# Shared-key attention on one core: transposed products in three banks, maxima turned on DVE, plain scores issued first

## Chip, cores and metric

The kernel runs on one core of one Trainium2 chip. The metric is the device time of one execution in microseconds, from runs of the compiled program; lower is better. The kernel before takes 4062.18 us, the median of three runs (4059.2 to 4066.68).

## What is computed

The reference is four transformer layers over x of shape [4, 512, 512]; each adds an attention and then a feed-forward part to x. The change touches the attention of the last two layers only, which is the same in both: 32 query heads of width 16 share 8 key/value heads, and keys and values are the context itself.

```python
def _L2_xattn_ref(q, k, v):
    NUM_Q_HEADS = 32
    NUM_KV_HEADS = 8
    ...
    qh = q.reshape(B, S, KV, G, D).transpose(0, 2, 3, 1, 4)
    kh = k.reshape(B, S, KV, D).transpose(0, 2, 1, 3)
    vh = v.reshape(B, S, KV, D).transpose(0, 2, 1, 3)
    scores = jnp.einsum('bkgsd,bktd->bkgst', qh, kh) / scale
    weights = jax.nn.softmax(scores, axis=-1)
    out = jnp.einsum('bkgst,bktd->bkgsd', weights, vh)
    return out.transpose(0, 3, 1, 2, 4).reshape(b, s, E)
```

The call adds this to x: `x = x + _L2_xattn_ref(_layernorm(x, axis=-1), ctx_512, ctx_512)`, and the same for layer 3.

## The kernel before

`stage_attend_shared` (L1385) is built twice, as at2 and at3. A **group** is one key/value head of one of the four batches with its four query heads, so there are 32 groups in a stage. A group has 16 **pairs** n = 0 to 15, each a tile of 128 tokens and one head, over 512 tokens.

Every score is made twice. The **plain** score of a pair (`scores`, L1521, matmul L1529) has queries down the partitions, and only serves to find each query's maximum over the keys: two pairs, n = 2m and 2m+1, fill one of two PSUM tiles of two banks, `score[m % 2]`, and DVE reduces the set m in one instruction (`max_set`, L1645, L1648). So pair 2m waits on PE until DVE has reduced set m - 2 (`maxed`). The **transposed** score (`scores_T`, L1534, matmul L1540) has keys down the partitions. Its query operand `qT` carries two more rows, the maxima split in a high and a low part, which meet rows of -1 in `kT`; so the maximum is already subtracted. ACT takes the exponential of each out of PSUM (L1628) into `probs`. Two banks, `scoreT[n % 2]`, serve the transposed products, so the one of pair n waits for the exponential of pair n - 2 (`exped`). The plain score of a pair sits in one half of the array's rows and the transposed one of the same pair in the other half.

`results(g, place, t)` (L1543, L1553) multiplies the four `probs` of one tile with the values, the fourth block of a group being issued in the next slot after pair LAST; such four products are called a results block below. ACT copies the accumulated result out (`move_res`, L1620), PE turns it with four transpositions (`turn_results`, L1565) into bank 7, and DVE divides by the sums (`finish`, L1661: a reciprocal L1663 and a product L1666).

The maxima take this path: DVE splits them (`split_maxima`, L1655, L1657), PE turns them by four transpositions into bank 7 as well (`turn_max`, L1560), ACT copies eight rows to `maxT` (`move_max`, L1615), and SP writes them with four DMAs into `qT` (`put_max`, L1495).

The order of work is written out by hand. One **slot** s does the transposed scores and results of group s and the plain scores and reductions of group s + 2. On PE a slot runs over the pairs, and these lines set it:

```python
    LAST, VALUES, MAX, RES = 1, (5, 9, 13), 5, 9
    ...
                    scores_T(s, place, j, n)
                    if ahead >= 2:
                        scores(s + 2, place + 2, j, n)
                    if n == LAST and not first:
                        results(s - 1, place + 3, TB - 1)
                    if n in VALUES:
                        results(s, place, VALUES.index(n))
```

`turn_max` stands after pair 5 (MAX) and `turn_results` after pair 9 (RES). On DVE a slot is the split of group s + 1's maxima, then eight reductions, with `finish(s - 1)` after the reduction of set (RES + 1) // 2 = 5. On SP a slot is the twelve loads of group s + 3 and then the four DMAs of `put_max`. Slots 1 to 24 run in a loop whose body holds eight of them; slots 30 and 31 have no plain scores.

Of the kernel before, what the change touches and what calls it, by code (L numbers as in the profile page):

```python
# [1384 lines left out]
def stage_attend_shared(k, nm, ctx_g, q_hi, q_lo, k_hi, k_lo, factor, queries):  # L1385
# [12 lines left out]
    LAST, VALUES, MAX, RES = 1, (5, 9, 13), 5, 9  # L1398
    with stage_room(k) as room:
        ctx, block = room.memory, room.block  # L1400

        def sb(name, shape, dt=F32):
# [8 lines left out]
        maxima, inv = sb("maxima", [P, TB, H]), sb("inv", [P, TB, H])  # L1411
        split = [sb(f"split{r}", [P, TB, P // 2, 2], F32R) for r in range(2)]
        maxT = [sb(f"maxT{r}", [2 * H, S]) for r in range(2)]
# [3 lines left out]
        (cleared, consts, spilled, scored, maxed, max_split, turned_max, max_moved, scoredT, exped, valued, vals_kept, res_moved, turned_res,  # L1417
         inv_made, finished, added) = k.sems(
            ctx, nm, "cleared consts spilled scored maxed max_split turned_max max_moved scoredT exped valued vals_kept res_moved turned_res "
# [29 lines left out]

        @block.vector  # L1450
        def _(dve):
            for r in range(SLOTS):
                dve.memset(kT[r][:, :].bitcast(F32), -1.0).then_inc(cleared, 1)
            for r in range(2):
                dve.memset(vals[r][:, :, :], 0.0).then_inc(consts, 1)
                dve.memset(split[r][:, :, :, :].bitcast(F32), 0.0).then_inc(consts, 1)
            dve.wait_ge(consts, 4)
# [13 lines left out]
        def _(sp):  # L1471
# [15 lines left out]
            def put_max(place, j, g):  # L1487
# [15 lines left out]
            put_max(0, 0, 0)  # L1503
            sp.wait_ge(spilled, 2 * B * DMA)

            def slot(s, place, j, ahead):
                if ahead >= 3:
# [3 lines left out]
                if ahead >= 1:  # L1511
                    put_max(place + 1, j, s + 1)
# [4 lines left out]
        def _(pe):  # L1517
# [16 lines left out]
            def scores_T(g, place, j, n):  # L1534
# [4 lines left out]
                pe.wait_ge(exped, PAIRS * g + n + 1)  # L1539
                pe.matmul(scoreT[n % 2][:, :], kT[r][half(h % 2, USED + 2), t * P:(t + 1) * P], qT[r][half(h % 2, USED + 2), h // 2, :],  # L1540
# [15 lines left out]
            def turn_max(g, place):  # L1556

                pe.wait_ge(max_split, 2 * (g + 1))
# [1342 lines left out]
```

## Time and profile before

| | |
|---|---|
| median of three runs | 4062.18 us |
| the profiled execution's own time | 4080.94 us |
| its span on the core | 4079.3 us |
| PE busy | 3337.4 us (82%) |
| DVE busy | 2324.2 us (57%) |
| ACT busy | 1934.3 us (47%) |
| granted PE clock over the span | 0.91 of full |
| reductions L1648, 512 of them | 623.9 us busy, 259.5 us idle before them |
| exponentials L1628, 1024 of them | 568.4 us busy, 368.0 us idle before them |
| transposed scores L1540, 1024 of them | 452.1 us busy, 177.8 us idle before them |

The shares are means over stages with other limits; the two attention stages run from about 1775 to 2276 us and from about 3140 to 3659 us of the span. The numbers behind a group of instructions are its busy time and the time that its engine stood idle just before one of them. A timeline row gives start and length in us, and in brackets the idle time of the engine before it and what ended it. The granted clock is 1.00 at 2.4 GHz and 0.50 at 1.2 GHz.

### The profile page before, as it was taken

The page shows a single profiled execution, that of the slowest core. Times are in us where ns is not written, and L with a number is a line of the kernel's source. Part 1 is how long each engine was busy: PE and PEld are TensorE (multiplying, and loading weights), DVE is VectorE, ACT ScalarE, POOL GpSimd, SP SyncE. Part 2 cuts the span into 40 slices and gives each one's busy share as a digit, 9 for nine tenths or more (in the row PEclk, how much of TensorE's full clock was granted, in tenths as well). Part 3 has the DMA queues.
Part 4 walks back from the last instruction along what each step waited for, and adds up shares of the span by engine and source line. Part 5 has one row for each costly group of instructions (what it writes and reads, how often), then busy time and mean ns, then how long its engine had stood idle before and what let it go on. Part 6 is the DMA issues. An engine that isn't in the chain of part 4 may idle for free. (4 is left out here: it accounts for less than half of the span.)

```text
span 4079.3 us, 62234 instructions
## 1 busy us (share of the span) xinstructions
PE 3337.4 (82%) x17174; PEld 2276.6 (56%) x17174; DVE 2324.2 (57%) x3679; ACT 1934.3 (47%) x3331; POOL 606.2 (15%) x901
## 2 busy tenths in 40 slices
PE   3359996899871999668888689899897788878998
PEld 2137775666551788533332367888775233326886
DVE  6954445455443343477777444566567676745565
ACT  5643333355530555346666433566433566654333
POOL 2410001544223000210000030122111000000000
PEclk7669998999985999869999799999997999989999
DMA  3424442400011333341111152567443211102223
GB/s 137 147 98 139 139 138 89 165 0 0 11 52 62 111 119 107 111 152 43 42 41 32 70 183 93 193 242 240 167 141 119 71 40 41 42 21 67 96 94 113
DMA packets 174475, 404.47 MB, mean 99 GB/s; under 512 B 28484, under 2 KB 28612, under 8 KB 173682
## 3 DMA queue, kind: packets, MB, share of 16 engines
q1 hardware_dynamic: 141010, 286.47, 22.0%
q0 software_dynamic: 22480, 96.23, 6.9%
q10 hardware_dynamic: 10864, 20.45, 1.3%
q8 instruction: 41, 0.67, 0.1%
q14 instruction: 80, 0.66, 0.1%
HBM read 312.32 MB, written 87.03 MB: 98 GB/s over the span
## 5 line engine op out<-in xcount | busy, mean ns | idle before, releaser
L1648 DVE TENSOR_REDUCE at_maxima<-psum 128x2 f32<-128x1024 f32 x512 | 623.9, 1223 | 259.5 <-PE psum L1529 241.8
L1628 ACT ACTIVATE at_probs<-psum 128x512 f32<-128x512 f32 x1024 | 568.4, 595 | 368.0 <-PE psum L1540 337.6
L1540 PE MATMUL psum<-at_qT,at_kT 50*128 50x512 f32 x1024 | 452.1, 491 | 177.8 <-ACT at_probs L1628 167.7
L1540 PEld LDWEIGHTS psum<-at_qT,at_kT 50*128 50x128 f32 x1024 | 175.9, 192 | 496.9 <-ACT at_probs L1628 438.6
L1529 PE MATMUL psum<-at_kT,at_qT 48*128 48x512 f32 x1024 | 431.4, 496 | 14.6 <-DVE at_maxima L1648 12.4
L573 PE MATMUL psum<-f_xT_hi,ffn_w_hi 128*128 x1024 | 406.8, 397 | 9.9 <-DVE f_xT_lo L313 2.8
L573 PE MATMUL psum<-f_xT_lo,ffn_w_hi 128*128 x1024 | 405.9, 396 | 0.0
L1553 PE MATMUL psum<-at_probs,at_vals 128*32 128x512 f32 x2048 | 292.7, 640 | 0.0
L590 PE MATMUL psum<-ffn_w_hi,ffn_hid_hi 128*128 128x512 f32 x768 | 269.3, 391 | 1.3 <-ACT ffn_hid_hi L636 1.3
L387 PE MATMUL psum<-ident,n_normed 128*128 128x128 f32 x448 | 95.5, 389 | 195.9 <-ACT n_normed L353 159.3
L478 ACT ACTIVATE ffn_w_hi<-ffn_w_raw 128x512 fp32r<-128x512 f32 x262 | 161.6, 633 | 157.3 <-PE psum L595 100.1
L573 PEld LDWEIGHTS psum<-f_xT_hi,ffn_w_hi 128*128 128x128 f32 x1024 | 194.0, 189 | 56.7 <-issue 12.1
L486 DVE TENSOR_TENSOR ffn_w_lo<-ffn_w_raw,ffn_w_hi 128x512 fp32r<-128x512 f32 x262 | 176.7, 686 | 76.1 <-ACT ffn_w_hi L478 75.9
L573 PEld LDWEIGHTS psum<-f_xT_lo,ffn_w_hi 128*128 128x128 f32 x1024 | 193.9, 189 | 44.5
L595 PE MATMUL psum<-ffn_w_hi,ffn_hid_lo 128*128 128x512 f32 x768 | 205.3, 389 | 0.0
L1325 DVE TENSOR_REDUCE at_maxima<-psum 128x1 f32<-128x128 f32 (+3 forms) x256 | 122.5, 489 | 141.9 <-PE psum L1135 138.3
L573 PE MATMUL psum<-f_xT_hi,ffn_w_lo 128*128 x512 | 202.5, 396 | 0.0
L592 PE MATMUL psum<-ffn_w_lo,ffn_hid_hi 128*128 128x512 f32 x512 | 199.5, 390 | 0.0
L387 PEld LDWEIGHTS psum<-ident,n_normed 128*128 128x128 f32 x448 | 79.8, 204 | 212.0 <-issue 147.8
L1529 PEld LDWEIGHTS psum<-at_kT,at_qT 48*128 48x128 f32 x1024 | 170.8, 194 | 28.5 <-DVE at_maxima L1648 22.7
L676 DVE TENSOR_TENSOR n_normed<-n_normed,psum 128x512 f32<-128x512 f32 (+1 forms) x88 | 60.4, 687 | 217.2 <-ACT n_normed L633 211.0
L1296 ACT ACTIVATE at_probs<-psum 128x512 f32<-128x512 f32 (+3 forms) x256 | 111.9, 438 | 136.9 <-PE psum L1149 136.7
(399 smaller groups left out, 7354.9 us busy)
## 6 DMA issues: line engine op xcount, KB each, us to landing
ffn_w_raw<-in_stream SPq DMA_DIRECT2D x262, 256.0 KB, 2.7
ffn_w_hi<-quantized SPq DMA_DIRECT2D x66, 512.0 KB, 3.5
ffn_w_hi<-quantized SPq DMA_DIRECT2D x65, 256.0 KB
at_qT<-q_hi SPq DMA_DIRECT2D x256, 64.0 KB, 2.2
ffn2a_w_raw<-in_shared2a SPq DMA_DIRECT2D x26, 512.0 KB
ffn2b_w_raw<-in_shared2b SPq DMA_DIRECT2D x26, 512.0 KB
qz_raw<-in_stream SPq DMA_DIRECT2D x17, 768.0 KB, 4.2
quantized<-qz_quant POOLq DMA_DIRECT2D x16, 768.0 KB, 3.5
```

The source lines that it names most:

```text
L387: mm = pe.transpose(turned_ps[u][:, c, :], normed[u][:, c * P:(c + 1) * P], k.ident[:, :])
L478: act.activation(hi[slot][:, :], raw[slot][:, :], ACT.Copy).then_inc(made, 1)
L486: dve.tensor_tensor(lo[slot][:, :], raw[slot][:, :], hi[slot][:, :].bitcast(F32), ALU.subtract).then_inc(made, 1)
L573: mm = pe.matmul(hid_ps[h][s][0:n, :], wt[s][:, w], xt[:, c, bass.ds(b * S, S)], start=(c == 0 and i == 0), stop=(c == DC - 1 and i == len ...
L590: pe.matmul(out[t][:, :], hid_hi[s][0:n, tok], w2_hi[s][0:n, :], start=first, stop=False)
L592: pe.matmul(out[t][:, :], hid_hi[s][0:n, tok], w2_lo[s][0:n, :], start=False, stop=False)
L595: mm = pe.matmul(out[t][:, :], hid_lo[s][0:n, t * P:(t + 1) * P], w2_hi[s][0:n, :], start=False, stop=last)
L1529: mm = pe.matmul(score[m % 2][:, 512 * (n % 2):512 * (n % 2) + S], qT[r][half(par, USED), jj, t * P:(t + 1) * P], kT[r][half(par, USED), : ...
L1540: pe.matmul(scoreT[n % 2][:, :], kT[r][half(h % 2, USED + 2), t * P:(t + 1) * P], qT[r][half(h % 2, USED + 2), h // 2, :], start=True, sto ...
L1553: pe.matmul(res[h * OW:(h + 1) * OW, :], vals[place % 2][:, t, :], probs[n % RING][:, :], start=(t == 0), stop=(t == TB - 1), tile_positio ...
L1628: act.activation(probs[n % RING][:, :], scoreT[n % 2][:, :], ACT.Exp, scale=factor).then_inc(exped, 1)
L1648: dve.tensor_reduce(maxima[:, t, 2 * jj:2 * jj + 2], score[m % 2].rearrange("p (h s) -> p h s", h=2), AX.X, ALU.max).then_inc(maxed, 1)
```

## The change

Three things change in `stage_attend_shared`; line numbers below that are not of the kernel before are those of the changed one.

1. Transposed products rotate through three banks, 4 to 6 (`turn_of`). `res` moves to bank 7. The turned results no longer have a bank of their own: they take the bank of the rotation that would be pair 8's, between pair 7 and pair 10. So pair n waits for the exponential of pair n - 3 (n - 2 for pairs 0, 1, 8, 9), and pair 10 waits for `finish`.
2. The maxima are turned on DVE, by a transposition of 32x32 blocks (L1652) into `across`. SP writes that to a DRAM scratch `tops` (`send_max`, L1495), waits for the landing, and `put_max` (L1506) gathers from `tops` into `qT` in four DMAs. PE's four transpositions and ACT's copy per group are gone.
3. The plain score of pair n is issued ahead of the transposed one. The positions in a slot are now LAST = 2, VALUES = (6, 10, 14), RES = 7, and `finish` follows the reduction of set (7 + 1) // 2 = 4.

```diff
-    LAST, VALUES, MAX, RES = 1, (5, 9, 13), 5, 9
+    LAST, VALUES, MOVE, RES = 2, (6, 10, 14), 2, 7
+    TURNS = 3
...
-        score, scoreT, res, turn = [room.psum[:, 1024 * m:1024 * m + 1024] for m in range(2)], room.banks[4:6], room.banks[6], room.tiles(7)
+        score, scoreT, res = [room.psum[:, 1024 * m:1024 * m + 1024] for m in range(2)], room.banks[4:4 + TURNS], room.banks[7]
+        turn = room.tiles(4 + (RES + 1) % TURNS)
...
+        def turn_of(n):
+
+            return (n if n <= RES else n + 1) % TURNS
...
+            def send_max(place, g):
+
+                sp.wait_ge(max_turned, g + 1)
+                sp.dma_start(tops[place % SLOTS, :, :], across[place % 2][:, :]).then_inc(max_out, DMA)
+
...
-                sp.wait_ge(max_moved, g + 1)
+                sp.wait_ge(max_out, DMA * (g + 1))
+                rows = tops[r, :, :].rearrange("(b h o t) i -> h o t b i", b=TB, h=H, o=2)
                 for jj in range(2):
                     for par in range(2):
                         at = HALF * par + USED
-                        row0 = 2 * (2 * jj + 1 - par)
-                        sp.dma_start(qT[r][at:at + 2, jj, :].bitcast(F32), maxT[place % 2][row0:row0 + 2, :]).then_inc(put[r], DMA)
+                        dst = qT[r][at:at + 2, jj, :].bitcast(F32).rearrange("o (t b i) -> o t b i", t=TB, b=TB)
+                        sp.dma_start(dst, rows[2 * jj + 1 - par]).then_inc(put[r], DMA)
...
             def slot(s, place, j, ahead):
+                if ahead >= 1:
+                    send_max(place + 1, s + 1)
                 if ahead >= 3:
...
-                pe.wait_ge(exped, PAIRS * g + n + 1)
-                pe.matmul(scoreT[n % 2][:, :], kT[r][half(h % 2, USED + 2), t * P:(t + 1) * P], qT[r][half(h % 2, USED + 2), h // 2, :],
+                if n < 2:
+                    pe.wait_ge(exped, PAIRS * g + n + 1)
+                elif n > 2:
+                    pe.wait_ge(exped, PAIRS * g + (n + 1 if RES < n < RES + TURNS else n))
+                if n == RES + TURNS and not is_first(g):
+                    pe.wait_ge(finished, g + 1)
+                pe.matmul(scoreT[turn_of(n)][:, :], kT[r][half(h % 2, USED + 2), t * P:(t + 1) * P], qT[r][half(h % 2, USED + 2), h // 2, :],
...
-                    scores_T(s, place, j, n)
                     if ahead >= 2:
                         scores(s + 2, place + 2, j, n)
+                    scores_T(s, place, j, n)
                     if n == LAST and not first:
                         results(s - 1, place + 3, TB - 1)
                     if n in VALUES:
                         results(s, place, VALUES.index(n))
-                    if n == MAX and ahead >= 1:
-                        pe.wait_ge(max_moved, s + 1)
-                        if not first:
-                            pe.wait_ge(finished, s)
-                        turn_max(s + 1, place + 1)
                     if n == RES and not first:
                         pe.wait_ge(res_moved, s)
-                        if ahead >= 1:
-                            pe.wait_ge(max_moved, s + 2)
-                        else:
-                            pe.wait_ge(finished, s)
+                        pe.wait_ge(exped, PAIRS * s + n + 1)
                         turn_results()
...
-                    if n == MAX + 1 and ahead >= 1:
-                        move_max(s + 1, place + 1, j)
...
+                if not (isinstance(g, int) and g < 2):
+                    dve.wait_ge(max_out, DMA * (g - 1))
+                dve.transpose(across[place % 2][:, :], split[:, :, :, :].rearrange("p h o t -> p (h o t)").bitcast(F32)).then_inc(max_turned, 1)
```

PE in the middle of a slot of the kernel before; L1540 is the transposed and L1529 the plain score, L1553 the results, L1565 the turned results. The rows begin with the two scores of pair 9:

```order
L1540 MATMUL psum<-at_qT,at_kT 128x512
L1529 MATMUL psum<-at_kT,at_qT 128x512
L1553 MATMUL psum<-at_probs,at_vals 32x512 x4
L1565 MATMUL psum<-ident,at_resT 128x128 x4
L1539 REGISTER_ALU
L1540 MATMUL psum<-at_qT,at_kT 128x512
L1528 REGISTER_ALU
L1529 MATMUL psum<-at_kT,at_qT 128x512
L1539 REGISTER_ALU
L1540 MATMUL psum<-at_qT,at_kT 128x512
L1529 MATMUL psum<-at_kT,at_qT 128x512
```

The same place in the changed kernel, where L1559 is the transposed and L1543 the plain score, L1572 the results and L1577 the turned results. The rows begin just behind the turning that follows pair 7, with pairs 8, 9 and 10, and end with a results block and the plain score of pair 11:

```order
L1542 REGISTER_ALU
L1543 MATMUL psum<-at_kT,at_qT 128x512
L1556 REGISTER_ALU
L1559 MATMUL psum<-at_qT,at_kT 128x512
L1543 MATMUL psum<-at_kT,at_qT 128x512
L1556 REGISTER_ALU
L1559 MATMUL psum<-at_qT,at_kT 128x512
L1542 REGISTER_ALU
L1543 MATMUL psum<-at_kT,at_qT 128x512
L1559 MATMUL psum<-at_qT,at_kT 128x512
L1572 MATMUL psum<-at_probs,at_vals 32x512 x4
L1543 MATMUL psum<-at_kT,at_qT 128x512
```

Before, a results block stood behind the odd pair of a set, so both plain scores of the set were out; now it stands behind the even pair, and the odd pair's plain score comes after the block. The last transposed score shown, pair 10's, is the one that waits for `finish`.

DVE in the changed kernel, from the split and the new transposition at a slot's head to `finish` (L1657, L1660) and the reduction behind it:

```order
L1646 CAST at_split<-at_maxima 128x4x4
L1647 ISA
L1648 TENSOR_TENSOR at_split<-at_maxima,at_split 128x4x4
L1649 REGISTER_ALU
L1651 REGISTER_ALU
L1652 STREAM_TRANSPOSE at_across<-at_split 128x32
L1638 REGISTER_ALU
L1639 TENSOR_REDUCE at_maxima<-psum 128x2 x2
```

```order
L1639 TENSOR_REDUCE at_maxima<-psum 128x2
L1657 RECIPROCAL at_inv<-psum 128x16
L1660 TENSOR_TENSOR at_result<-psum,at_inv 128x256
L1638 REGISTER_ALU
L1639 TENSOR_REDUCE at_maxima<-psum 128x2
```

`finish` moved ahead by one reduction, from behind the sixth to behind the fifth, and the transposition is new.

## Rows read from the trace of the kernel before

**Rows 1.** All transposed scores: count, ns min/median/max, first and last start.

```profile
L1540 PE MATMUL psum<-at_qT,at_kT x1024: 386/495/793, 1793.3 to 3655.0; 50*128 50x512 f32 x171
```

**Rows 2.** PE's timeline, 1904 to 1926 us: start, length, engine, line, tiles, idle before.

```profile
1904.36 0.50 PE L1529 MATMUL psum<-at_kT,at_qT 48*128 48x512 f32 x1
1904.79 1.06 PE L1553 MATMUL psum<-at_probs,at_vals 128*32 128x512 f32 x8
1905.78 0.66 PE L1565 MATMUL psum<-ident,at_resT 128*128 128x128 f32 x4
...
1906.37 0.73 PE L1529 MATMUL psum<-at_kT,at_qT 48*128 48x512 f32 x2
...
1910.66 0.50 PE L1540 MATMUL psum<-at_qT,at_kT 50*128 50x512 f32 x1 [0.45 <-ACT at_probs L1628]
...
1925.19 0.50 PE L1540 MATMUL psum<-at_qT,at_kT 50*128 50x512 f32 x1 [0.45 <-ACT at_probs L1628]
```

**Rows 3.** DVE's timeline, 1904 to 1909 us.

```profile
1904.92 1.23 DVE L1648 TENSOR_REDUCE at_maxima<-psum 128x2 f32<-128x1024 f32 x1 [0.65 <-PE psum L1529]
1907.18 1.23 DVE L1648 TENSOR_REDUCE at_maxima<-psum 128x2 f32<-128x1024 f32 x1 [1.04 <-PE psum L1529]
1908.33 0.25 DVE L1663 RECIPROCAL at_inv<-psum 128x16 f32<-128x16 f32 x1
1908.61 0.42 DVE L1666 TENSOR_TENSOR at_result<-psum,at_inv 128x256 f32<-128x256 f32 x1
```

**Rows 4.** Timeline of all engines at 1789 us, before slot 0.

```profile
1789.08 2.36 DVE L1648 TENSOR_REDUCE at_maxima<-psum 128x2 f32<-128x1024 f32 x2 [0.40 <-PE psum L1529]
...
1790.36 0.80 PE L1529 MATMUL psum<-at_kT,at_qT 48*128 48x512 f32 x2 [0.82 <-DVE at_maxima L1648]
```

**Rows 5.** Groups by line, 1910.6 to 1925.2 us: busy, mean ns, idle before.

```profile
L1648 DVE TENSOR_REDUCE at_maxima<-psum 128x2 f32<-128x1024 f32 x9 | 11.0, 1224 | 3.9 <-PE psum L1529 3.4
```

**Rows 6.** SP's timeline of the same slot: the first load, the four puts.

```profile
1910.39 0.34 SPq L1482 DMA_DIRECT2D at_qT<-q_hi  x1
...
1918.38 2.43 SPq L1495 DMA_DIRECT2D at_qT<-at_maxT  x4
```

**Rows 7.** PE's timeline at three longer waits.

```profile
1928.33 0.78 PE L1540 MATMUL psum<-at_qT,at_kT 50*128 50x512 f32 x1 [1.16 <-ACT at_probs L1628]
...
3304.78 0.50 PE L1540 MATMUL psum<-at_qT,at_kT 50*128 50x512 f32 x1 [1.19 <-ACT at_probs L1628]
...
3424.88 0.50 PE L1540 MATMUL psum<-at_qT,at_kT 50*128 50x512 f32 x1 [0.99 <-ACT at_probs L1628]
```

**Rows 8.** Stretches behind them: us, busy (PE, PEld, DVE, ACT, POOL), PEclk, DMA, GB/s.

```profile
1928.40:1935.20 6.80, 6.53 (x24) 2.65 (x24) 2.45 (x2) 3.04 (x6) 0.00 (x0) 0.50 0.19 49
...
3307.40:3310.70 3.30, 3.30 (x16) 1.31 (x16) 1.22 (x1) 0.60 (x1) 0.00 (x0) 0.50 0.06 20
...
3426.90:3437.00 10.10, 9.63 (x36) 3.55 (x38) 3.93 (x4) 3.85 (x8) 0.00 (x0) 0.50 0.06 17
```

**Rows 9.** PE's timeline in slot 30 of at3, where no plain scores are.

```profile
3628.38 0.79 PE L1540 MATMUL psum<-at_qT,at_kT 50*128 50x512 f32 x1
3629.10 1.93 PE L1553 MATMUL psum<-at_probs,at_vals 128*32 128x512 f32 x8
3630.97 1.12 PE L1565 MATMUL psum<-ident,at_resT 128*128 128x128 f32 x4
```

**Rows 10.** PE's timeline: slot 30 and last turning of at2, slot 0, 30, last turning of at3.

```profile
2240.12 0.90 PE L1540 MATMUL psum<-at_qT,at_kT 50*128 50x512 f32 x2 [0.54 <-ACT at_probs L1628]
...
2275.85 0.66 PE L1565 MATMUL psum<-ident,at_resT 128*128 128x128 f32 x4 [0.69 <-ACT at_resT L1620]
...
3170.56 0.79 PE L1540 MATMUL psum<-at_qT,at_kT 50*128 50x512 f32 x1 [9.78 <-DMA at_qT<-at_maxT]
...
3618.34 0.90 PE L1540 MATMUL psum<-at_qT,at_kT 50*128 50x512 f32 x2 [0.54 <-ACT at_probs L1628]
...
3658.40 0.66 PE L1565 MATMUL psum<-ident,at_resT 128*128 128x128 f32 x4 [0.69 <-ACT at_resT L1620]
```

More of the change, by code:

```diff
@@ L1455, in _ @@
                 dve.memset(vals[r][:, :, :], 0.0).then_inc(consts, 1)
-                dve.memset(split[r][:, :, :, :].bitcast(F32), 0.0).then_inc(consts, 1)
-            dve.wait_ge(consts, 4)
+            dve.wait_ge(consts, 2)
             for r in range(2):
@@ L1554, in results @@
                               start=(t == 0), stop=(t == TB - 1), tile_position=(0, h * OW), skip_group_check=True).then_inc(valued, 1)
-            def turn_max(g, place):
-                pe.wait_ge(max_split, 2 * (g + 1))
-                for t in range(TB):
-                    mm = pe.transpose(turn[:, t, :], split[place % 2][:, t, :, :].rearrange("p c o -> p (c o)").bitcast(F32), k.ident[:, :])
-                mm.then_inc(turned_max, 1)
             def turn_results():
@@ L1566, in turn_results @@
                 mm.then_inc(turned_res, 1)
-            pe.wait_ge(consts, 6)
+            pe.wait_ge(consts, 4)
             for g in range(2):
@@ L1571, in _ @@
                     scores(g, g, 0, n)
-                    if g == 1 and n == MAX:
+                    if g == 1 and n == 0:
                         pe.wait_ge(made, before + N // P)
-                        turn_max(0, 0)
             def slot(s, place, j, ahead):
@@ L1608, in _ @@
             act.sem_inc(exped, 2)
-            def move_max(g, place, j):
-                act.wait_ge(turned_max, g + 1)
-                if not (isinstance(g, int) and g < 2):
-                    act.wait_ge(put[(place + 2) % SLOTS], PUTS * DMA * (use(place - 2, j) + 1))
-                act.activation(maxT[place % 2][:, :], turn[0:2 * H, :, :].rearrange("p t q -> p (t q)"), ACT.Copy).then_inc(max_moved, 1)
             def move_res(g):
@@ L1627, in slot @@
                     act.wait_ge(valued, PAIRS * s + n + 1)
-                    act.activation(probs[n % RING][:, :], scoreT[n % 2][:, :], ACT.Exp, scale=factor).then_inc(exped, 1)
-                    if n == LAST + 1 and not is_first(s):
+                    act.activation(probs[n % RING][:, :], scoreT[turn_of(n)][:, :], ACT.Exp, scale=factor).then_inc(exped, 1)
+                    if n == MOVE and not is_first(s):
                         move_res(s - 1)
-                    if n == MAX + 1 and ahead >= 1:
-                        move_max(s + 1, place + 1, j)
             all_slots(act, slot)
@@ L1642, in _ @@
             dve.sem_inc(finished, 1)
-            dve.wait_ge(consts, 6)
+            dve.wait_ge(consts, 4)
             def max_set(g, m):
@@ L1647, in max_set @@
                 dve.wait_ge(scored, SETS * g + m + 1)
-                dve.tensor_reduce(maxima[:, t, 2 * jj:2 * jj + 2], score[m % 2].rearrange("p (h s) -> p h s", h=2), AX.X, ALU.max).then_inc(maxed, 1)
+                dve.tensor_reduce(maxima[:, 2 * jj:2 * jj + 2, t], score[m % 2].rearrange("p (h s) -> p h s", h=2), AX.X, ALU.max).then_inc(maxed, 1)
             def split_maxima(g, place):
-                hi, lo = split[place % 2][:, :, 0:H, 0], split[place % 2][:, :, 0:H, 1]
+                hi, lo = split[:, :, 0, :], split[:, :, 1, :]
                 dve.wait_ge(maxed, 2 + SETS * (g + 1))
-                if not (isinstance(g, int) and g < 2):
-                    dve.wait_ge(turned_max, g - 1)
+                if not (isinstance(g, int) and g < 1):
+                    dve.wait_ge(max_turned, g)
                 dve.tensor_copy(hi, maxima[:, :, :]).then_inc(max_split, 1)
```

27 lines of the change are left out of this document (13 added, 14 removed).

## The prediction

> **What bounds the kernel now.** I read the page's groups first, then the timelines of PE and DVE over one slot in the middle of at2, and then the granted clock around the few slots that are longer. The transposed scores run from 1793.3 us on [rows 1]. One slot takes 14.53 us, from one first transposed score to the next [rows 2], and both ends of it wait 0.45 us for an exponential. That is the present bound: with two banks PE waits for ACT, ACT for PE. DVE isn't it; in that slot it waits 3.4 us for plain scores [rows 5]. No engine is full, so what a change of order gives depends on which waits it chains together. The 60 slots with plain scores take 2240.12 - 1793.31 = 446.8 us in at2 and 3618.34 - 3170.56 = 447.8 us in at3 [rows 1, 10], 894.6 in all or 14.91 each, since a few are longer.
>
> **What it removes.** Third bank: the waits of PE for exponentials go. The maxima's turning on PE goes as well, four transpositions; the like ones of the results take 0.59 us, from 1905.78 to 1906.37 [rows 2]. All that was on PE's path. So a slot could shrink. What is late next is the exchange of plain scores and reductions.
>
> **What it chains.** In the new order each results block stands between the even and the odd plain score of a set. DVE can't reduce the set until the block is through, and the plain score two sets on can't start until DVE is done, since it uses the same buffer. Four such rings follow one another in a slot. Three are alike: last pair to results block 0.43, from 1904.36 to 1904.79; block 0.99, to 1905.78 [rows 2]; a plain score that started alone to its reduction 0.56, 1904.36 to 1904.92 [rows 2, 3]; reduction to the plain score that waits for it 1.28, 1789.08 to 1790.36 [rows 4]. That is **3.26 us**. These three lead from pair 2 to pair 6, from pair 10 to pair 14, and from pair 14 to pair 2 of the next slot.
>
> The fourth, from pair 6 to pair 10, is longer, for it holds the new wait of pair 10 for `finish`. It is 0.43 and block 0.99; pair 7 to the turning 0.43; turning 0.59; pair 8's plain score to the reduction of set 4 0.81, as from 1906.37 to 1907.18 [rows 2, 3]; that reduction, reciprocal and product 1.15 + 0.28 + 0.42 [rows 3], and 0.05 for the signal (1.28 less the 1.23 of a reduction [rows 3, 4]), so 1.90. Sum **5.15 us**. Slot: 3 x 3.26 + 5.15 = **14.93 us**, nearly what it is now: the 60 slots come to 896 us, +1. In the wait for `finish`, plain score 10 is already out, pair 10's transposed score blocks the results block, and plain score 11 stands behind that; DVE and ACT run dry too. PE idles from the end of score 10 to the signal, some 1.5 us: 0.81 + 1.90 = 2.71 from pair 8 on, less three scores (two in 0.73, one alone 0.50 [rows 2]).
>
> **What the idle does to the clock.** In these stages PE waits of 1.16, 1.19 and 0.99 us [rows 7] were followed by stretches at 1.2 GHz of 6.8, 3.3 and 10.1 us [rows 8], while the usual waits of 0.45 [rows 2] mostly leave it at 2.4. The new wait is longer than any of the three and comes in every slot. At 1.2 GHz the pieces are 0.72 for pair to block and 1.87 for the block [rows 9], 0.79 instead of 0.50 for a score [rows 9, 2], so 0.85 for 0.56; DVE's stay. A ring of the first kind takes 0.72 + 1.87 + 0.85 + 1.28 = 4.72. In the fourth I scale 0.59 and 0.81 by 0.79/0.50, having no row of them: 0.72 + 1.87 + 0.72 + 0.93 + 1.28 + 1.90 = 7.42. Slot all at 1.2 GHz: 3 x 4.72 + 7.42 = 21.6. So a microsecond at the low clock loses 1 - 14.93/21.6 = 0.31. With the mean of the three stretches, 6.7 us, the slot gets 2.1 longer: **17.0 us**. Bounds: one stretch of 3.3 gives 15.95, one of 10.1 gives 18.06.
>
> In the Trainium skill, "TensorE: Matmul & The Clock Gate", section "HAM oscillation — how this bites in real kernels", the throttling comes of waits longer than any in my sum. By it the clock would stay and the slot be the 14.93 of rival 1. The trace speaks against it: rows 7 and 8. The same page's section "A second HAM failure mode: psum-queue depth-cycling" has short idles between groups of products swing the clock; by that rule, the trace agrees.
>
> **The rest.**
> - Slots 30 and 31 have no plain scores and take, with the last turning, 35.7 us in at2 and 40.1 in at3 [rows 10], partly waiting for exponentials. With three banks PE is left as the bound. At 1.2 GHz four transposed scores and a block take 0.54 (0.34 between pairs, scaled as above) + 0.72 + 1.87 = 3.1; four of them and a turning of 0.93 are 13.4, two slots 27, and 4 for the last block, copy and turning (estimate): 31. Gain 5 + 9 = 14 us.
> - The transposition on DVE: nearest rows are a reciprocal of 16 columns, 0.25, and a product of 256, 0.42 [rows 3]; it has 32 columns. I take 0.25, hidden: it comes before the first reduction of a slot, which isn't in a ring, and DVE waits 3.4 us per slot [rows 5]. If 0.2 of it came through, +12 us; a gain it can't be.
> - ACT loses a copy per group; it waits anyway: 0.
> - The maxima through DRAM. SP's twelve loads take under 8.0 us (1910.39 to 1918.38), four puts 2.43 [rows 6]. Counted from pair 2, the last reduction began at -1.28 and takes 1.15, split and transposition some 0.8, so the send goes out near 0.7. With 0.6 for it (a quarter of the puts), loads end by 9.3 and puts by 11.7. The next slot starts 1.5 before its pair 2 (0.56 + 1.28 less the 0.34 between two pairs), at 13.4, or at 15.5 in a 17.0 us slot. That leaves 1.7 or 3.8 us for landing; now the puts end at 1920.81, 4.4 before a slot that doesn't wait for them [rows 6, 2]. I take it as hidden; if it isn't, rival 4.
> - Start of the stages: in at3 slot 0 already waits 9.78 us for the puts [rows 10], behind the spills; one more round trip costs about 3 there and 1 in at2: +4.
> - The causes of the waits in rows 7 stay: 0.7 us more than usual, four times: +3.
>
> **Sum.** 60 x 17.0 = 1020, less 894.6, is +125; +3 +4 - 14 gives **+118 us**. It is worked out against one profiled execution (4080.94 us, span 4079.3); that stands 18.8 us over the median of 4062.18. I carry the difference over: 4062 + 118 = about **4181 us**. The bounds 15.95 and 18.06 give +55 and +182: 4118 and 4244.
>
> **Rivals.**
> 1. The clock holds. Then 60 x 14.93 = 896, and the low stretches that there are now remain, (14.91 - 14.53) x 60 = 23: +24 + 4 - 14 = +14, **4076 us**. For it: the usual waits are harmless. Against: rows 7 and 8. Its own bounds, 0.15 us per slot, reach to no difference.
> 2. The other side: the rings don't form, because set 4 and `finish` are done when PE gets to pair 10, and DVE's waits vanish: 14.53 - 3.4 + 0.2 = 11.3 us per slot, 678 + 23 - 895 = -194, with the rest -204: **about 3860 us**. For it: the waits for exponentials really go. Against: the score of pair 9 is issued only two scores ahead of pair 10's transposed one, and the reduction between takes 1.23. It decides when the four rings add up to less than 14.53 at the full clock, that is if I have 0.40 too much.
> 3. The clock never comes back within the stages: 60 x 21.6 = 1296, +401 - 7: **4456 us**. Against: after each stretch of rows 8 it rose.
> 4. A new wait at the slot's head: pieces of 128 bytes double the puts' issue, 2.4 us, and landing takes as long again as allowed, so that pair 0 waits about 1 us: +60 over the forecast, 4241. Against: 3.8 us of slack.
>
> **Chances.** Forecast 0.75, rival 1 0.11, rival 2 0.06, rival 3 0.04, rival 4 0.04. The range reaches from rival 1 to the forecast's upper bound: 4074 to 4246. What a measurement of this kernel can tell from no change is about 0.2%, 8 us. Faster by more: rival 2, 0.06. Within: the lower third of rival 1, 0.03. Slower: 0.91.
>
> **What would show it.** Right: transposed scores of pair 10 waiting over 1 us, once per slot, with `finish` (L1660) as releaser; reductions idle about 2 us behind each block; slots of 16 to 18 us; a granted clock swinging inside every slot, about 0.80 in the mean of the two stages (6.7 of 17.0 us at half); no waits for exponentials. Wrong: a clock near 1.00 with slots of 15 us (rival 1), slots under 14.5 (rival 2), or first scores of a slot waiting for a DMA (rival 4).

## The result, and the profile after

The changed kernel takes **4301.4 us**, median of four runs (4295.6 to 4317.55), beside 4060.69 us for the kernel before (4053.97 to 4066.68): a ratio of 1.060, 95% interval 1.0565 to 1.0634. It is slower, as forecast, but by 241 us instead of 118, and the time lies above the range of 4074 to 4246. Its profiled execution took 4295.6 us with a span of 4294.0, and the granted clock over the span fell from 0.91 to 0.84.

The costliest groups of the page of the changed kernel; [rows 1] answer to the L1559 line:

```profile
L1639 DVE TENSOR_REDUCE at_maxima<-psum 128x2 f32<-128x1024 f32 x512 | 612.0, 1220 | 480.9 <-PE psum L1543 477.5
L1621 ACT ACTIVATE at_probs<-psum 128x512 f32<-128x512 f32 x1024 | 567.5, 598 | 581.5 <-PE psum L1559 574.1
L1559 PE MATMUL psum<-at_qT,at_kT 50*128 50x512 f32 x1024 | 552.8, 627 | 116.5 <-DVE at_result L1660 91.9
L1543 PE MATMUL psum<-at_kT,at_qT 48*128 48x512 f32 x1024 | 527.2, 615 | 78.6 <-DVE at_maxima L1639 69.3
```

Reductions and exponentials cost about what they did, 612 and 568 us, but DVE and ACT now stand idle for 481 and 582 us (260 and 368 before), nearly all of it waiting for scores. The scores of PE are what got longer: 627 ns on the mean, where the median was 495 before [rows 1]. The waits for exponentials have gone from the top; in their place stand 91.9 us of waits for the product of `finish` (L1660), in 62 of the 64 slots: 1.48 us each, or 1.44 as a mean over all slots.

PE's timeline at one such wait, in slot 8 of at2:

```profile
1947.98 0.79 PE L1543 MATMUL psum<-at_kT,at_qT 48*128 48x512 f32 x1 [0.46 <-DVE at_maxima L1639]
1948.06 0.79 PE L1559 MATMUL psum<-at_qT,at_kT 50*128 50x512 f32 x1
1948.78 1.93 PE L1572 MATMUL psum<-at_probs,at_vals 128*32 128x512 f32 x8
...
1952.28 0.50 PE L1543 MATMUL psum<-at_kT,at_qT 48*128 48x512 f32 x1
...
1955.05 0.47 PE L1559 MATMUL psum<-at_qT,at_kT 50*128 50x512 f32 x1 [1.80 <-DVE at_result L1660]
1955.45 1.94 PE L1572 MATMUL psum<-at_probs,at_vals 128*32 128x512 f32 x8
```

A score takes 0.79 us, then 0.50 from 1952.28 on: the clock has just risen. Pair 10 then waits 1.80 us for `finish`, and the results block behind it takes 1.94 again. The stretches around it in the windows view (busy us of PE, PEld, DVE, ACT, POOL; granted clock, DMA share, GB/s), then both stages from slot 0 to slot 30:

```profile
1914.50:1952.10 37.60, 34.15 (x126) 12.10 (x122) 18.93 (x23) 17.32 (x31) 1.20 (x3) 0.50 0.14 33
1952.10:1955.50 3.40, 1.60 (x12) 0.72 (x14) 2.41 (x4) 1.08 (x2) 0.41 (x1) 1.00 0.02 4
1955.50:1958.90 3.40, 3.40 (x15) 0.99 (x14) 0.76 (x1) 1.32 (x3) 0.31 (x1) 0.50 0.02 5
1958.90:1972.60 13.70, 10.89 (x60) 4.40 (x62) 10.01 (x13) 7.84 (x16) 0.75 (x2) 1.00 0.17 47
...
1796.60:2357.70 561.10, 481.01 (x2027) 171.31 (x2028) 317.69 (x384) 281.82 (x508) 27.88 (x58) 0.68 0.13 33
3278.00:3832.80 554.80, 474.51 (x2028) 169.53 (x2028) 317.61 (x384) 281.69 (x508) 27.90 (x58) 0.69 0.13 33
```

The longest stretch of [rows 8] was 10.1 us; here 37.6 us pass at 0.50, more than a slot and a half, though PE is busy for 34.15 of them. Over both stages the clock is 0.68 to 0.69; in the kernel before it was 0.97 over the same slots.

The two spans are 214.7 us apart, less than the 241 of the medians: the profiled execution of the kernel before took 20 us more than its median, that of the changed one 6 less. Where the 214.7 us lie (working from the first transposed scores of slots 0 and 30 and the last turnings, as in [rows 10]):

| part | before | after | difference |
|---|---|---|---|
| up to slot 0 of at2 | 1793.3 | 1796.6 | +3.3 |
| slots 0 to 29 of at2 | 446.8 | 561.1 | +114.3 |
| slots 0 to 29 of at3 | 447.8 | 554.8 | +107.0 |
| slots 30, 31 and the last turning, both stages | 75.8 | 77.0 | +1.2 |
| between the stages, to slot 0 of at3 | 894.7 | 881.7 | -13.0 |
| behind at3 | 420.9 | 422.8 | +1.9 |

All of the loss is in the 60 slots: 18.6 us each instead of 14.91. The stretch between the stages is code that the change does not touch, and it differs by 30 us between two kernels below whose last slots are nearly the same (from slot 31 to slot 0 of at3, 927.7 us in keep_busy and 897.9 in keep_busy_all); I read nothing into its 13.

### The profile page after: what moved, and what is told of

Its sections match the earlier page's. It is cut to its first block and busy times, and to the rows that moved or that the text cites. A ratio compares the mean times of both kernels' runs of the same rounds, so it can differ in the third digit from the quotient of the medians.

```text
span 4294.0 us, 61624 instructions
## 1 busy us (share of the span) xinstructions
PE 3558.6 (83%) x16914; PEld 2338.5 (54%) x16918; DVE 2323.6 (54%) x3739; ACT 1919.3 (45%) x3267; POOL 606.6 (14%) x901
## 5 line engine op out<-in xcount | busy, mean ns | idle before, releaser
L1639 DVE TENSOR_REDUCE at_maxima<-psum 128x2 f32<-128x1024 f32 x512 | 612.0, 1220 | 480.9 <-PE psum L1543 477.5
L1559 PE MATMUL psum<-at_qT,at_kT 50*128 50x512 f32 x1024 | 552.8, 627 | 116.5 <-DVE at_result L1660 91.9
L1543 PE MATMUL psum<-at_kT,at_qT 48*128 48x512 f32 x1024 | 527.2, 615 | 78.6 <-DVE at_maxima L1639 69.3
L1543 PEld LDWEIGHTS psum<-at_kT,at_qT 48*128 48x128 f32 x1024 | 234.2, 259 | 552.1 <-issue 332.9
L1572 PE MATMUL psum<-at_probs,at_vals 128*32 128x512 f32 x2048 | 410.2, 883 | 0.0
L1559 PEld LDWEIGHTS psum<-at_qT,at_kT 50*128 50x128 f32 x1024 | 234.4, 257 | 211.8 <-issue 136.6
```

Source lines behind the costliest of these rows:

```text
L1543: mm = pe.matmul(score[m % 2][:, 512 * (n % 2):512 * (n % 2) + S], qT[r][half(par, USED), jj, t * P:(t + 1) * P], kT[r][half(par, USED), : ...
L1559: pe.matmul(scoreT[turn_of(n)][:, :], kT[r][half(h % 2, USED + 2), t * P:(t + 1) * P], qT[r][half(h % 2, USED + 2), h // 2, :], start=True ...
L1572: pe.matmul(res[h * OW:(h + 1) * OW, :], vals[place % 2][:, t, :], probs[n % RING][:, :], start=(t == 0), stop=(t == TB - 1), tile_positio ...
L1639: dve.tensor_reduce(maxima[:, 2 * jj:2 * jj + 2, t], score[m % 2].rearrange("p (h s) -> p h s", h=2), AX.X, ALU.max).then_inc(maxed, 1)
```

## Experiments

All times are medians with their own runs of the kernel before beside them on the same chip. "Low" is the share of the 60 slots at the lower clock, "wait" the mean wait of pair 10's transposed score (pair 12's in the last row).

| kernel | us | before | ratio, interval | slot at2 / at3 | low at2 / at3 | wait |
|---|---|---|---|---|---|---|
| the change | 4301.4 | 4060.7 | 1.060 [1.0565, 1.0634] | 18.70 / 18.49 | 0.64 / 0.62 | 1.44 |
| keep_busy | 4224.4 | 4077.8 | 1.034 [1.0287, 1.0399] | 17.55 / 17.23 | 0.47 / 0.42 | 0.21 |
| keep_busy_all | 4196.0 | 4063.3 | 1.035 [1.0281, 1.0423] | 16.39 / 17.41 | 0.29 / 0.45 | about 0.2 |
| keep_busy_full | 4095.9 | 4085.7 | 1.002 [0.9997, 1.0040] | 15.39 / 15.14 | 0.08 / 0.04 | 0.00 |
| full_elsewhere | 4367.1 | 4062.0 | 1.075 [1.0735, 1.0771] | 20.35 / 20.05 | 0.68 / 0.64 | 1.35 |
| t_first | 4310.1 | 4085.7 | 1.057 [1.0527, 1.0615] | 18.90 / 18.83 | 0.63 / 0.64 | 1.89 |
| finish_early | 4022.4 | 4077.8 | 0.987 [0.9850, 0.9885] | 13.96 / 14.01 | 0.04 / 0.06 | 0.21 |
| blocks_odd | 3951.8 | 4077.8 | 0.969 [0.9675, 0.9711] | 12.97 / 13.01 | 0.02 / 0.03 | 0.39 |
| both | 3893.7 | 4063.3 | 0.958 [0.9550, 0.9610] | 12.24 / 12.38 | 0.03 / 0.08 | 0.00 |
| blocks_3 | 3856.2 | 4063.3 | 0.949 [0.9451, 0.9521] | 11.63 / 11.72 | 0.03 / 0.05 | 0.03 |
| blocks_3_t_first | 3875.7 | 4085.7 | 0.950 [0.9469, 0.9535] | 11.83 / 11.74 | 0.06 / 0.05 | 0.23 |
| maxima_only | 4030.0 | 4077.8 | 0.988 [0.9863, 0.9896] | 14.19 / 13.90 | 0.15 / 0.10 | - |
| before_wait | 4379.8 | 4063.3 | 1.077 [1.0734, 1.0805] | 20.27 / 19.93 | 0.64 / 0.59 | 1.92 |

### 1. Is it the idle, or the order of the work?

**keep_busy** fills pair 10's wait with products whose result is overwritten:

```diff
                 if n == RES + TURNS and not is_first(g):
+                    m = n + 1
+                    pe.wait_ge(exped, PAIRS * g + m)
+                    for _ in range(4):
+                        pe.matmul(scoreT[turn_of(m)][:, :], kT[r][half(m % H % 2, USED + 2), m // H * P:(m // H + 1) * P],
+                                  qT[r][half(m % H % 2, USED + 2), m % H // 2, :], start=True, stop=True)
                     pe.wait_ge(finished, g + 1)
```

> The changed kernel, with four more matmuls per slot put on PE just ahead of pair 10's wait for finish: they make pair 11's transposed product four times in its bank, and it is made again in its turn, so the output is the same. The wait and every ring stay. Theory (the idle PE in that wait brings the clock down, and the low clock is the cost): PE now works in most of the 1.44 us, the granted clock of the two stages rises from 0.67 to over 0.9, slots fall from 18.6 us to 15.0 and the time from 4301 us to about 4080, although more is computed. Rival (the time is in the waits and in the longer way of the maxima, and the clock only follows): no less than 4290 us; with 4 x 0.4 us of added work per slot up to 4400.

Measured: 1.034, between the two theories. Slots that stay at the high clock take 15.0 us, against 14.93 in the sum of the prediction, but others took up to 21.8. The wait is all but gone and less than half of the loss with it. PE's timeline of this kernel at a fall, and the two stretches there:

```profile
1985.97 1.19 PE L1561 MATMUL psum<-at_qT,at_kT 50*128 50x512 f32 x4
1987.44 0.79 PE L1564 MATMUL psum<-at_qT,at_kT 50*128 50x512 f32 x1 [0.28 <-DVE at_result L1665]
1988.16 1.93 PE L1577 MATMUL psum<-at_probs,at_vals 128*32 128x512 f32 x8
```

```profile
1984.00:1987.40 3.40, 3.09 (x15) 1.65 (x13) 3.04 (x4) 1.69 (x3) 0.00 (x0) 1.00 0.32 87
1987.40:1995.00 7.60, 7.10 (x27) 2.08 (x29) 2.36 (x2) 2.77 (x5) 0.72 (x1) 0.50 0.02 3
```

PE was busy for 3.09 of 3.40 us and idle for 0.28, and the clock fell all the same. So length of idle is not all that counts.

**keep_busy_all** adds two such products ahead of the plain scores of pairs 2, 6 and 14 too, to fill the waits in the other three rings.

```diff
+                    if n in (2, 6, 14) and not first:
+                        t, h, r = n // H, n % H, place % SLOTS
+                        pe.wait_ge(exped, PAIRS * s + n)
+                        for _ in range(2):
+                            pe.matmul(scoreT[turn_of(n)][:, :], kT[r][half(h % 2, USED + 2), t * P:(t + 1) * P],
+                                      qT[r][half(h % 2, USED + 2), h // 2, :], start=True, stop=True)
                     if ahead >= 2:
                         scores(s + 2, place + 2, j, n)
```

> The kernel of keep_busy with the other three waits of PE in a slot filled too: two extra products each just ahead of the plain scores of pairs 2, 6 and 14, which wait for a reduction. They make that pair's transposed product in its bank early, and it is made again in its turn; output the same. keep_busy brought the share of the low clock from 0.63 to 0.45 and had slots of exactly 15.0 us at the full clock beside others of up to 21.8. Theory (every idle stretch of PE counts, not that of the long wait alone): the clock stays high, slots of 15.0 to 15.3 us, 0 to 60 us over the kernel before. Rival (what holds the low clock is the kind of product and not the idle time, or the low clock is not what costs): no less than keep_busy's 3.4% over the kernel before.

Measured: 1.035, no better. PE is busy 467.94 of 491.40 us in at2 (0.95), and yet the clock was low for 0.29 of the time there and 0.45 in at3; the longest slots took 22.4 us. Filling more idle with this kind of product does not help.

**keep_busy_full** fills pair 10's wait again, now with two products that use all 128 rows of the array where the scores use 48 or 50:

```diff
+                    pe.wait_ge(exped, PAIRS * g + n + 1)
+                    for _ in range(2):
+                        pe.matmul(scoreT[turn_of(n + 1)][:, 0:384], k.ident[:, :], probs[(n - 2) % RING][:, 0:384], start=True, stop=True)
                     pe.wait_ge(finished, g + 1)
```

> The change, with two redundant full-array products (128 x 128 by 384 columns) issued ahead of pair 10's wait for DVE's finish, in place of the four half-array products of the earlier run, which took the waiting to 0.21 us a slot and still left slots of up to 21.8 us. Theory A, it matters to the clock which products fill the wait: with whole-array work once a slot the granted clock stays at 2.4 GHz nearly throughout, the slots are 15.0 to 15.3 us, 60 of them 60 x (15.15 - 14.91) = +15 us, and the time is 4060 to 4110 us. Theory B, the kind does not matter, only that the slot as a whole holds too little of the rest: as the four half-array products, slots of 17.2 to 17.6 us on the mean and 4200 to 4240 us.

Measured: 1.002, interval 0.9997 to 1.0040, theory A. PE's timeline of this kernel in slot 10 of at2:

```profile
1952.09 1.07 PE L1575 MATMUL psum<-at_probs,at_vals 128*32 128x512 f32 x8
...
1955.33 1.07 PE L1575 MATMUL psum<-at_probs,at_vals 128*32 128x512 f32 x8
...
1958.64 1.06 PE L1575 MATMUL psum<-at_probs,at_vals 128*32 128x512 f32 x8
...
1961.88 1.56 PE L1560 MATMUL psum<-at_probs,ident 128*128 128x384 f32 x4
1963.37 0.50 PE L1562 MATMUL psum<-at_qT,at_kT 50*128 50x512 f32 x1
1963.79 0.64 PE L1575 MATMUL psum<-at_probs,at_vals 128*32 128x512 f32 x4
```

```profile
1950.00:1965.00 15.00, 13.22 (x74) 5.07 (x74) 10.67 (x13) 9.39 (x17) 0.97 (x2) 1.00 0.17 41
1796.90:2258.50 461.60, 408.18 (x2144) 156.71 (x2144) 317.76 (x384) 280.14 (x508) 27.93 (x58) 0.96 0.16 40
```

The products take 1.56 us, about what pair 10 would have waited. This kernel does all that the change does, and more; its blocks come 3.24, 3.31 and 5.15 us apart, the very rings of the prediction, and it is level with the kernel before. So the rings with their waits cost next to nothing while the clock holds, and practically the whole 6% is the clock. Where it does fall in this kernel, it is isolated: for 6.8 us in slot 9 of at2 and 10.2 in slot 17, places where it falls in the kernel before and in finish_early below too. They are the first slots of rounds of the eight-slot loop, and after the one in slot 9 the clock held for over 100 us in all three.

**full_elsewhere** has the same two products, but ahead of pair 5's transposed score, and leaves pair 10's wait alone.

```diff
+                if n == 5 and not is_first(g):
+                    for _ in range(2):
+                        pe.matmul(scoreT[turn_of(n)][:, 0:384], k.ident[:, :], probs[(n - 3) % RING][:, 0:384], start=True, stop=True)
```

> The change with the same two redundant full-array products (128 x 128 by 384 columns, 1.56 us in the kernel that filled pair 10's wait with them) at another place: ahead of pair 5's transposed score, with pair 10's wait for the finish left as it is. The plain score of pair 6 waits 0.84 us for a reduction in that kernel, and may hide part of them. Theory A, the clock fell for want of whole-array work in a slot, wherever it stands: the clock holds, the slots are 14.93 + 1.56 - 0.84 = 15.7 us at most, 60 x 0.8 = +47 us, 4080 to 4140 us. Theory B, it is pair 10's wait that must be filled, and the kind of product that fills it: that wait stays at 1.4 us or more, the share of low clock near 0.6, slots of 18.5 to 19.5 us and 4280 to 4350 us. Between them, both count: 4150 to 4250 us.

Measured: 1.075, theory B, and the slots even longer than it expected (20.2 on the mean). They lock to one pattern:

```profile
1961.90:1968.70 6.80, 5.70 (x29) 2.30 (x26) 4.72 (x6) 3.51 (x7) 0.00 (x0) 0.99 0.22 59
1968.70:1982.40 13.70, 12.79 (x46) 4.31 (x46) 5.96 (x9) 5.43 (x10) 0.96 (x2) 0.51 0.07 18
1982.40:1989.20 6.80, 5.67 (x27) 2.30 (x26) 4.74 (x6) 3.86 (x7) 0.00 (x0) 0.99 0.21 62
```

```profile
1962.21 1.56 PE L1561 MATMUL psum<-at_probs,ident 128*128 128x384 f32 x4
...
1969.14 0.76 PE L1562 MATMUL psum<-at_qT,at_kT 50*128 50x512 f32 x1 [1.47 <-DVE at_result L1663]
1969.84 1.93 PE L1575 MATMUL psum<-at_probs,at_vals 128*32 128x512 f32 x8
```

The clock falls in pair 10's wait and comes back 13.7 us later, every 20.5 us. Whole-array work keeps it up where it stands in the wait, and not where it stands ahead of pair 5, the one other place tried. Nor is it shown to bring the clock back: it rose at about 1962.1, a tenth of a microsecond ahead of the products at 1962.21, too near to call either way.

**t_first** undoes the order of the two scores alone:

```diff
+                    scores_T(s, place, j, n)
                     if ahead >= 2:
                         scores(s + 2, place + 2, j, n)
-                    scores_T(s, place, j, n)
```

> The change with the transposed scores issued ahead of the plain ones again, as before the change; banks and the turned maxima as changed. Theory A, pair 10's wait for the finish is what lets the clock fall and the order of the two products has little to do with it: the wait stays over 1 us a slot, the share of low clock near 0.6, slots 18.0 to 18.8 us, 4260 to 4310 us. Theory B, the order is what lets it fall: slots 14.6 to 15.2 us, no longer than before, 4040 to 4090 us.

Measured: 1.057, theory A. With the plain scores behind the transposed ones pair 10 waits 1.89 us, and the clock is low for 0.63 and 0.64 of the time, as in the change. The order of the two scores is not what lets it fall. The rest of the change's third part, the positions of the results blocks and of `finish`, is varied in part 2 below.

**before_wait** puts such a wait into the kernel before, which has neither third bank nor rings:

```diff
+                if n == 12 and not is_first(g):
+                    pe.wait_ge(finished, g + 1)
```

> The kernel before with one wait more and nothing else: the transposed score of pair 12 waits for finish of the group before, which is about 1.5 us later than PE gets there. Theory: the wait costs its own 1.5 us, a slot of 16.0 us, and the clock falls in most slots on top, another 2 us or more: 60 x 3.5 = 210 us over the kernel before, granted clock of the stages under 0.85. Rival (idle PE of this length costs its own length): 60 x 1.5 = 90 us over.

Measured: 1.077, the theory's way, but 316 us over the kernel before where it had 210. PE's timeline of this kernel at the wait:

```profile
1953.62 0.47 PE L1542 MATMUL psum<-at_qT,at_kT 50*128 50x512 f32 x1 [2.06 <-DVE at_result L1668]
...
1954.57 1.93 PE L1555 MATMUL psum<-at_probs,at_vals 128*32 128x512 f32 x8
```

Slots grow from 14.91 to 20.1 us, by 5.2, of which the wait is 1.9 at most; the rest I put down to the low clock, 0.62 of the time: at the price of the prediction, 0.31, that is 12.4 x 0.31 = 3.8 us (estimate). One wait of two microseconds in a slot is enough for it.

### 2. Taking away the wait or the rings

**finish_early** lets `finish` go one reduction earlier, and nothing else:

```diff
-                    if m == (RES + 1) // 2 and not is_first(s):
+                    if m == RES // 2 and not is_first(s):
```

> The changed kernel with finish one reduction earlier on DVE, behind the fourth instead of the fifth; nothing else. Theory (pair 10's wait for finish closes the fourth ring): finish no longer has the reduction of pairs 8 and 9 in front of it, the ring falls from 5.15 to 0.43 + 0.99 + 0.56 + 1.15 + 0.75 = 3.88 us, pair 10 waits about 0.3 us, a slot takes 3 x 3.26 + 3.88 = 13.7 us and the clock stays high: about 4061 - 60 x 1.25 = 3985 us, or 3970 if the low stretches of the kernel before go too. Rival (the maxima's way over DRAM, or the third bank itself, costs the time): over 4200 us.

Measured: 0.987, slots of 13.8 us, 55 us under the kernel before where the theory had some 75. DVE's timeline of this kernel in slot 11 of at2, then PE's:

```profile
1958.61 1.23 DVE L1639 TENSOR_REDUCE at_maxima<-psum 128x2 f32<-128x1024 f32 x1 [0.96 <-PE psum L1543]
1959.76 0.25 DVE L1657 RECIPROCAL at_inv<-psum 128x16 f32<-128x16 f32 x1
1960.04 0.42 DVE L1660 TENSOR_TENSOR at_result<-psum,at_inv 128x256 f32<-128x256 f32 x1
1960.38 1.22 DVE L1639 TENSOR_REDUCE at_maxima<-psum 128x2 f32<-128x1024 f32 x1
```

```profile
1957.09 1.06 PE L1572 MATMUL psum<-at_probs,at_vals 128*32 128x512 f32 x8
...
1960.61 0.47 PE L1559 MATMUL psum<-at_qT,at_kT 50*128 50x512 f32 x1 [0.22 <-DVE at_result L1660]
1961.01 1.06 PE L1572 MATMUL psum<-at_probs,at_vals 128*32 128x512 f32 x8
```

The product ends 1.2 us earlier, and the fourth ring is 3.92 us instead of 5.15 (1957.09 to 1961.01). One index takes the ratio from 1.060 to 0.987, some 300 us: about 72 by the shorter ring (60 x 1.2, an estimate) and the rest by the clock, which is low for 0.05 of the time instead of 0.63.

**blocks_odd** puts the results blocks back behind odd pairs, so that both plain scores of a set are out ahead of a block. The wait for `finish` stays.

```diff
-    LAST, VALUES, MOVE, RES = 2, (6, 10, 14), 2, 7
+    LAST, VALUES, MOVE, RES = 1, (5, 9, 13), 2, 7
```

> The changed kernel with the results blocks behind the odd pairs again, 1, 5, 9 and 13, as in the kernel before; finish, banks, maxima and the plain score first as changed. Theory (a block between the two plain scores of a set makes DVE wait for the block and PE for DVE): three of the four rings go, and the block behind pair 9 stands in the wait for finish, so that PE idles 0.6 us of it; slots of 13.0 us, clock mostly high: about 3950 us. Rival (only the wait for finish matters, and blocks between scores cost nothing since the four rings add up to the old slot): not under 4150 us, for pair 10 still waits for finish.

Measured: 0.969, slots of 12.9 us; pair 10 waits 0.39. **both** joins the edits of the last two:

> The changed kernel with the results blocks behind pairs 1, 5, 9 and 13 and with finish behind the fourth reduction: the two undone together. Alone they gave slots of 12.9 and 13.8 us. Theory: no block stands between the two plain scores of a set and pair 10 finds finish done; what is left is PE's own work and DVE's eight reductions, about 11.9 us a slot, clock high: 60 x 3.0 = 180 us under the kernel before, about 3885 us against 4078. Rival (the two hide the same wait, so the second gives nothing): 126 us under, as with the blocks alone.

Measured: 0.958, slots of 12.0: 170 us under the kernel before, near the theory's 180 and clear of the rival's 126. **blocks_3** has the blocks a pair further back than the change, behind odd pairs too, with the early `finish`.

```diff
-    LAST, VALUES, MOVE, RES = 2, (6, 10, 14), 2, 7
+    LAST, VALUES, MOVE, RES = 3, (7, 11, 15), 3, 7
...
-                    if m == (RES + 1) // 2 and not is_first(s):
+                    if m == RES // 2 and not is_first(s):
```

> As in both, but the results blocks behind pairs 3, 7, 11 and 15 and the copy of the results after the exponential of pair 3: each block has its four exponentials done two pairs earlier. Theory: as both or a little less, 11.6 us a slot, since PE no longer waits for the third exponential ahead of a block: 180 to 200 us under the kernel before. Rival (a later block holds back the probs ring, so ACT waits for PE): slower than both.

Measured: **0.949**, interval 0.9451 to 0.9521, slots of 11.2 to 11.4 us in the steady part: the best of all. **blocks_3_t_first** is that kernel with the edit of t_first.

> The kernel of three value blocks with the finish after the reduction, with the transposed scores ahead of the plain ones. What the plain-first order gives where the clock holds: Theory A, it puts the values' product behind the exponential a little later, so that undoing it costs 0.1 to 0.3 us a slot: 60 x 0.2 = +12 us, 3860 to 3885 us. Theory B, it costs or gives nothing: 3850 to 3862 us.

Measured: 0.950, with an interval that overlaps. Slots are 0.1 us longer on the mean, 7 us in all, and pair 10 waits 0.23 us where it waited 0.03. That leans to theory A at half its size, but two ratios on different chips do not separate it from nothing.

### 3. The maxima's new path alone

**maxima_only** is the kernel before with the maxima turned on DVE and sent through DRAM; two banks, old order, blocks where they were. The diff to the kernel before, cut to its core:

```diff
-    LAST, VALUES, MAX, RES = 1, (5, 9, 13), 5, 9
+    LAST, VALUES, MOVE, RES = 1, (5, 9, 13), 2, 9
...
-                    if n == MAX and ahead >= 1:
-                        pe.wait_ge(max_moved, s + 1)
-                        if not first:
-                            pe.wait_ge(finished, s)
-                        turn_max(s + 1, place + 1)
...
+                if ahead >= 1:
+                    send_max(place + 1, s + 1)
...
+                dve.transpose(across[place % 2][:, :], split[:, :, :, :].rearrange("p h o t -> p (h o t)").bitcast(F32)).then_inc(max_turned, 1)
```

> The kernel before with the second part of the change alone: maxima turned on DVE and brought to the queries over DRAM; two banks, transposed score first, old positions. Theory: PE loses four transpositions (0.59 us) and ACT a copy that delays one exponential by 0.4 us, per slot, and nothing comes in their place: slots of 13.55 us, about 4061 - 60 x 0.98 + 4 = 4006 us. Rival (the way over DRAM is late in each slot, or DVE's transposition is on the path): 4061 us or more, with the first transposed score of a slot waiting for a DMA.

Measured: 0.988, slots of 13.5 us where the clock holds, and 14.05 with the rest. So the second part of the change is a gain of 1.2% by itself. In the change the transposition takes 0.21 us on DVE, and the send and the puts sit beside other work (send, first and last loads, puts on SP in slot 9):

```profile
1963.57 0.35 SPq L1495 DMA_DIRECT2D tops<-at_across  x1
1964.23 0.32 SPq L1487 DMA_DIRECT2D at_qT<-q_hi  x1
...
1970.02 2.56 SPq L1506 DMA_DIRECT2D at_qT<-tops  x4
```

## Why the prediction was right in direction and wrong in size

**The rings: right.** The three alike came out at 3.24 and 3.31 us (3.26 in the sum) and the fourth at 5.15 (5.15) in keep_busy_full; slots at the full clock are 15.0 us (14.93). In the change itself `finish` released pair 10 2.00 us after the start of set 4's reduction (1953.05 on DVE to 1955.05), where the sum had 1.90.

**Pair 10's wait: right.** 1.44 us on the mean, 1.5 forecast, once a slot, released by L1660 as named.

**What a slot costs at 1.2 GHz: right.** The slots that are wholly low take 21.8 us (21.6 forecast); with (18.6 - 14.93) / 11.7 = 0.31 per low microsecond the rate held too (11.7 is the mean of the two stages' 12.0 and 11.4 below).

**How long it stays low: wrong, and this is the step that failed.** "With the mean of the three stretches, 6.7 us, the slot gets 2.1 longer" took one stretch a slot, and its length from isolated drops, [rows 8], where nothing like the wait followed for slots on end. The three that it took were not short ones either: nine drops begin in the 60 slots of the kernel before, of 3.4 to 10.2 us, 4.9 on the mean. In the change the clock was low for 12.0 us of a slot in at2 and 11.4 in at3. Putting 11.7 in place of 6.7 gives 14.93 + 11.7 x 0.31 = 18.6 us, the slot measured, and 60 x 1.6 = +96 us on the sum. The bound of 10.1 was one stretch per slot too; in the change there are fewer drops than slots, 43 in the 60, but they last for 703 us in all, 16 each on the average, and the longest, 37.6 us, run across slots. Of the 123 us that the forecast was short of the medians' 241, these 96 are the greater part; 26 are the two profiled executions' distance from their medians, and no term of the sum. The forecast of 0.80 for the granted clock was 0.68 for the same reason. Rival 3, a clock that never comes back, had the slot at 21.6 us, and the truth lay over half way from 14.93 to that; the range stopped at 18.06 a slot.

**What does it, as far as the runs tell.** Shown: with the wait filled by whole-array products the loss is gone (keep_busy_full); with those products ahead of pair 5 and the wait left open it is not (full_elsewhere); with the wait shortened to 0.21 us by an earlier `finish` it is gone (finish_early); with one wait added to the kernel before it appears (before_wait). So pair 10's wait sets it off. Open: why four products that use half of the array's rows, filling the same wait, leave over half of the loss (keep_busy), when finish_early, with the same 0.21 us of waiting and nothing in its place, holds the clock. The redundant products all lie in one half of the rows, one behind the other, while a pair's two scores run in both halves side by side; that they count for less is my reading, and no run here separates it from their timing in the slot. The Trainium skill, "TensorE: Matmul & The Clock Gate", section "HAM oscillation — how this bites in real kernels", puts such falls down to idle gaps longer than any in these slots. By that rule the change would have been rival 1, 4076 us; the measured 4301, with waits of 1.44 us on the mean and 1.80 in the timeline above, speaks against it here.

**The smaller terms.** Start of at2: +3.3, and at3's slot 0 waits 12.69 us for the puts instead of 9.78, +2.9 (+4 forecast for both). Transposition 0.21 us, hidden, 0.25 forecast. Puts: hidden, rival 4 did not come; waits for them stand at the starts of the stages alone. Slots 30 and 31: no gain, +1.2 us instead of -14. The sum had put at3's two slots at the low clock with no wait; one score and one block there are as priced (0.79 and 1.93 us), but two slots and the last turning take 38.5 us in both stages, not 31. The piece that was wrong shows in slot 30 of at2:

```profile
2370.62 1.22 PE L1559 MATMUL psum<-at_qT,at_kT 50*128 50x512 f32 x3
2372.10 0.79 PE L1559 MATMUL psum<-at_qT,at_kT 50*128 50x512 f32 x1 [0.26 <-ACT at_probs L1621]
2372.82 1.93 PE L1572 MATMUL psum<-at_probs,at_vals 128*32 128x512 f32 x8
```

With three banks the fourth transposed score still waits for an exponential, and starts 1.48 us behind the first, not 0.54. Each block with its four scores takes 4.07 us instead of 3.13, and eight of them are the 7.5 us that the sum lacked.

**Rival 2** had its arithmetic right for another kernel: no rings, 11.3 us a slot and about 3860 us. That is blocks_3, 11.2 to 11.4 us and 3856. What it wanted was not 0.40 us of slack but blocks behind odd pairs and `finish` one reduction earlier; its picture of that state, DVE without waits, holds there: DVE is busy 280.81 of 310 us (from 1830 us on).

## What to carry to other kernels

Where a change puts a PE wait of over a microsecond into every turn of a loop, price the loop at both clocks, and take the price at the full clock only as the lower bound. In the four kernels here with waits of 1.35 to 1.92 us in every slot the clock was low for 0.59 to 0.68 of the time, and the slot of the change came out over half way between the two prices: the length of an isolated drop says little about drops that come again in every slot or two. Look for the instruction behind which a wait ends (here `finish` behind the fifth reduction), since moving it by one place was worth some 300 us. And put products that share one buffer with a reduction on the same side of any long block.

## What was unexpected of the hardware

- The clock stayed at 1.2 GHz for 37.6 us with PE busy 34.15 of them (0.91); in keep_busy, where redundant products fill most of the wait, even for 61.4 us (from 2137.7 on) with PE busy 58.62 of them (0.95). Being busy with these products did not bring it back sooner.
- It fell after 3.40 us in which PE was busy for 3.09 (0.91), in keep_busy, and all but held in finish_early, where PE was busy 34.37 us of 40 (from 1930 us on), 0.86, at a clock of 0.98.
- Adding 1.56 us of whole-array products to a slot made the kernel 5.5% faster than the change in one place (ratios 1.002 and 1.060) and 1.4% slower in another (1.075).
- The clock can lock to the loop: 6.8 us high and 13.7 us low in each slot of 20.5 in full_elsewhere, for over twenty slots on end.
